# Converting the FFN weights inside tile 0 instead of ahead of it, and routing from the uncentred activations

## What is computed

```python
x = L0_attn_x
# block 1
h = ln(x);  spec = h @ W_to.T                     # 2*256 channels, real and imaginary
# per channel: state = state*decay + 0.1*u, rotated by a fixed angle, clipped to +-10
h = spectral_out @ W_from.T;  x2 = x + 0.1*h
h = gelu(ln(x2) @ W_ffn1.T + b1) @ W_ffn2.T + b2  # 4096 hidden
x = layernorm(x + (x2 + 0.1*h))
# block 2: mixture of experts, every expert computed densely, weighted by combine
logits = h @ router_weight.T                      # 8 columns
top_v, top_i = top_k(softmax(logits), 2);  top_v = top_v / top_v.sum()
gate, up = split(h @ gu.T);  out = silu(gate) * up @ dp.T
acc = acc + w[:, None] * out                      # over the 8 experts
x = layernorm(x + acc)
```

## Time and profile before

| | |
|---|---|
| runs shown | 5669.15 and 5701.72 us, median 5685.43 |
| profiled execution | 5680.6 us, span of its slowest core 5679.0 us |
| spans of the eight cores | 5626.9 to 5679.0 us |
| mean granted TensorE clock per core | 0.884 to 0.890 |
| TensorE, busy share of the span | 73% |
| VectorE, ScalarE, POOL | 35%, 18%, 8% |
| HBM | 641.87 MB read, 83.89 MB written |

### The profile page before, as it was taken

How to read it: one execution, slowest core, us unless ns; L and a number is a source line. 1 busy time by engine, 2 the same in 40 slices (tenths; PEclk the granted TensorE clock), 3 DMA queues, 4 the chain that set the end, 5 groups by cost and what they waited for, 6 DMA issues and landing times.

```text
span 5679.0 us, 55831 instructions; the slowest of 8 cores (5626.9 to 5679.0 us)
## 1 busy us (share of the span) xinstructions
PE 4162.6 (73%) x17824; PEld 1767.4 (31%) x17824; DVE 1979.9 (35%) x2879; ACT 1046.9 (18%) x1559; POOL 467.1 (8%) x391
## 2 busy tenths in 40 slices
PE   0028566665789768986789679987789578987797
PEld 0003222222334323332334233333334233433343
DVE  2032443222353324432353324431443325332333
ACT  0112311123111212112211212112201221122111
POOL 0000100000100002000100002000101001000210
PEclk9969788787899888997899789998899789988899
DMA  4722566662333242332333143332333233323242
GB/s 109 226 94 89 185 208 215 235 235 101 113 111 141 75 148 97 124 135 89 110 113 134 59 148 112 126 119 104 111 112 141 85 123 111 132 91 134 103 142 97
DMA packets 180314, 729.40 MB, mean 128 GB/s; under 512 B 28865, under 2 KB 28993, under 8 KB 112450
## 3 DMA queue, kind: packets, MB, share of 16 engines
...
HBM read 641.87 MB, written 83.89 MB: 128 GB/s over the span
## 4 chain that ended last, share of the span: by engine, by line
PE 63%; DVE 16%; DMA 6%; ACT 5%; SPq 5%; issue 3%; DVEq 1%; ACTq 1%; POOL 0%; POOLq 0%
PE PB L787 28%; PE PB L827 14%; PE PB L629 8%; PE PB L662 8%; SPq L257 4%; DMA RING<-guT 3%; ACT RING L286 2%; DVE ZS L442 2%; DVE PB L415 1%; DVE UPE L800 1%; PE PB L394 1%; PE PB L602 1%; DVE PRD L806 1%; DVEq L139 1%; DMA RING<-w1T 1%
## 5 line engine op out<-in xcount | busy, mean ns | idle before, releaser
L787 PE MATMUL PB<-BFIN,RING 128*128 128x512 bf16 x8192 | 1894.8, 394 | 173.3 <-ACT RING L286 113.4
L787 PEld LDWEIGHTS PB<-BFIN,RING 128*128 128x128 bf16 x8192 | 818.6, 101 | 1230.3 <-issue 372.8
L827 PE MATMUL PB<-PRD,RING 128*128 128x512 bf16 x4096 | 973.1, 400 | 226.9 <-DVE PRD L806 139.9
L629 PE MATMUL PB<-BFIN,RING 128*128 128x512 bf16 x2048 | 498.8, 404 | 388.2 <-DMA RING<-scr_w 223.8
L800 DVE TENSOR_TENSOR UPE<-PB,CBE 128x512 f32<-128x512 f32 x512 | 354.2, 692 | 1047.1 <-PE PB L787 969.4
L827 PEld LDWEIGHTS PB<-PRD,RING 128*128 128x128 bf16 x4096 | 412.7, 102 | 782.1 <-issue 360.6
L833 DVE TENSOR_TENSOR ACC<-PB,ACC 128x512 f32<-128x512 f32 x512 | 354.2, 692 | 693.3 <-PE PB L827 667.5
L806 POOL TENSOR_TENSOR PRD<-SG,UPE 128x512 bf16<-128x512 bf16 x256 | 297.1, 1160 | 2905.1 <-DVE UPE L800 2853.2
L794 ACT ACTIVATE SG<-PB 128x512 bf16<-128x512 f32 x512 | 303.6, 597 | 1034.9 <-PE PB L787 1027.5
L662 PE MATMUL PB<-G,RING 128*128 128x512 bf16 x2048 | 453.1, 379 | 0.0
L629 PEld LDWEIGHTS PB<-BFIN,RING 128*128 128x128 bf16 x2048 | 208.3, 102 | 677.2 <-issue 464.8
...
## 6 DMA issues: line engine op xcount, KB each, us to landing
...
RING<-scr_w SPq DMA_DIRECT2D x128, 1024.0 KB, 5.0
...
RING<-guT SPq DMA_DIRECT2D x256, 256.0 KB, 5.6
...
RING<-dpT SPq DMA_DIRECT2D x128, 256.0 KB, 5.4
...
```

Of the source, the lines that this page charges most:

```text
L629: mmm = opi("tensor", "T", lambda E, k=k, fc4=fc4, b=b, slot=slot: E.matmul(PB[b][:], slot[:, k * 512 + fc4 * 128: k * 512 + (fc4 + 1) * 1 ...
L787: mmm = opi("tensor", "T", lambda E, k=k, fc4=fc4, b=b, slot=slot, BFIN=BFIN: E.matmul(PB[b][:], slot[:, k * 512 + fc4 * 128: k * 512 + (f ...
L827: mmm = opi("tensor", "T", lambda E, k=k, oc4=oc4, b=b, slot=slot: E.matmul(PB[b][:], slot[:, k * 512 + oc4 * 128: k * 512 + (oc4 + 1) * 1 ...
```

## The change

Four things are changed.

1. `prewarm` is removed. The slabs of w1 and w2 are no longer converted ahead of tile 0; `emit_slab_load` finds no key for them in tile 0 and converts them there, inside FFN1 and FFN2, as it does for the expert slabs. The chain of tile 0 follows the router load directly.
2. In the twopass LN the squares go to the other activation buffer (`SQB`), and ScalarE no longer waits for the sum matmuls before it squares.
3. The router's matmuls take the uncentred bf16 cast in place of the normalized one. `RT` gets a ninth column of ones per chunk, which gives the token's sum; 32 matmuls of one column on the squares give the sum of squares. From these, eight small VectorE instructions and one small ScalarE square root make mean and reciprocal deviation per token and correct the logits by the column sums of the router weights (`SRB`, computed once at start-up with eight small matmuls). The ScalarE copy of the logits is gone. The POOL cast of the router weights becomes eight.
4. Pass 1 (the normalization into `BFIN`) is emitted behind the router's gating and not ahead of it. The first eight expert matmuls wait for it chunk by chunk.

At the end SyncE waits for all the DMA semaphores and not only for that of the output.

```diff
@@ -86,7 +87,7 @@
         CBE = sb("CBE", [128, T])
         WTO = sb("WTO", [128, KC * 512], BF16)
         WFR = sb("WFR", [128, 4 * 1024], BF16)
-        RT = sb("RT", [128, KC * NE], BF16)
+        RT = sb("RT", [128, KC * 9], BF16)
         RING = sb("RING", [128, 4 * 4096], BF16)
         ONESB = sb("ONESB", [128, 128], BF16)
         ONER = sb("ONER", [1, T], BF16)
@@ -99,6 +100,7 @@
         LDV = sb("LDV", [128, 2]); FRV = sb("FRV", [128, 2])
         DEC = sb("DEC", [128, 2]); PI2 = sb("PI2", [128, 1])
         LGS = sb("LGS", [128, 32])
+        SRB = sb("SRB", [128, 8])
         CMB = sb("CMB", [128, 32])
         CTE = sb("CTE", [8, T], BF16)
         MX4 = ZS[:, 0:32]; WW4A = ZS[:, 32:36]; WW4B = ZS[:, 36:40]
@@ -150,6 +152,9 @@
 
         def xc(buf, k, width=T):
             return buf[:, k * width:(k + 1) * width]
+
+        bank_free = [None] * 8
+        bank_ready = [None] * 8
 
         NRS = 4
         ring_free = [None] * NRS
@@ -326,8 +331,18 @@
         for kk in range(KC):
             ms_rt_rd = slot_dma(jr, lambda E, d=slot_r.bitcast(F32)[:, kk * 8:(kk + 1) * 8], s=rtR[kk]: E.dma_start(out=d, in_=s))
         w("gpsimd", ms_rt_rd)
-        ms_rt = opi("gpsimd", "G", lambda E, s=slot_r.bitcast(F32)[:, 0:64]: E.tensor_copy(out=RT[:], in_=s))
+        ms_rt = None
+        for kk in range(KC):
+            ms_rt = opi("gpsimd", "G", lambda E, kk=kk, s=slot_r.bitcast(F32)[:, kk * 8:(kk + 1) * 8]: E.tensor_copy(out=RT[:, kk * 9:kk * 9 + 8], in_=s))
         ring_set_free(jr, ms_rt)
+        ms_rto = opi("vector", "V", lambda E: E.memset(RT[:].rearrange("p (k e) -> p k e", k=KC)[:, :, 8], 1.0))
+        w("tensor", [ms_rt, ms_b2c, ms_rto])
+        ms_srb_mm = None
+        for kk in range(KC):
+            ms_srb_mm = opi("tensor", "T", lambda E, kk=kk: E.matmul(PB[6][:, 0:8], ONESB[:], RT[:, kk * 9:kk * 9 + 8], start=(kk == 0), stop=(kk == KC - 1)))
+        w("scalar", ms_srb_mm)
+        ms_srb = opi("scalar", "S", lambda E: E.activation(out=SRB[:], in_=PB[6][:, 0:8], func=AF.Copy))
+        bank_free[6] = ms_srb
 
         scr_ready = {}
 
@@ -354,8 +369,6 @@
 
 
 
-        bank_free = [None] * 8
-        bank_ready = [None] * 8
 
         def emit_slab_load(dram_ap, key):
             if key not in scr_ready:
@@ -383,6 +396,10 @@
             cast_ms = [None] * KC
             sq_ms = [None] * KC
             mmS_ms = [None] * KC
+            SQB = BFINS[1 - bfin_p] if twopass else BFIN
+            sq_p = (1 - bfin_p) if twopass else bfin_p
+            if twopass:
+                w("scalar", bfin_user[sq_p])
             for k in range(KC):
                 if per_chunk:
                     w("scalar", src_ready[k])
@@ -393,16 +410,19 @@
             for k in range(KC):
                 mmS_ms[k] = opi("tensor", "T", lambda E, k=k: E.matmul(PB[0][:], ONESB[:], xc(BFIN, k), start=(k == 0), stop=(k == KC - 1)))
             for k in range(KC):
-                w("scalar", mmS_ms[k])
-                sq_ms[k] = opi("scalar", "S", lambda E, k=k: E.activation(out=xc(BFIN, k), in_=src(k), func=AF.Square))
+                if not twopass:
+                    w("scalar", mmS_ms[k])
+                sq_ms[k] = opi("scalar", "S", lambda E, k=k: E.activation(out=xc(SQB, k), in_=src(k), func=AF.Square))
             w("tensor", bank_free[1])
             mmQ_last = None
             for k in range(KC):
                 w("tensor", sq_ms[k])
-                mmQ_last = opi("tensor", "T", lambda E, k=k: E.matmul(PB[1][:], ONESB[:], xc(BFIN, k), start=(k == 0), stop=(k == KC - 1)))
+                mmQ_last = opi("tensor", "T", lambda E, k=k: E.matmul(PB[1][:], ONESB[:], xc(SQB, k), start=(k == 0), stop=(k == KC - 1)))
             bank_ready[0] = mmS_ms[KC - 1]
             bank_ready[1] = mmQ_last
-            bfin_user[bfin_p] = mmQ_last
+            bfin_user[sq_p] = mmQ_last
+            if twopass:
+                bfin_user[bfin_p] = None
             w("vector", bank_ready[0])
             opi("vector", "V", lambda E: E.tensor_scalar(out=MEANT[:], in0=PB[0][:], scalar1=float(1.0 / D), scalar2=None, op0=OP.mult))
             opi("vector", "V", lambda E: E.tensor_tensor(out=ZS[:, 0:T], in0=MEANT[:], in1=MEANT[:], op=OP.mult))
@@ -417,12 +437,16 @@
             f_ms = [None] * KC
             if twopass:
                 w("vector", st.get("p2_done"))
-                opi("vector", "V", lambda E: E.tensor_copy(out=RSTD[:], in_=PB[1][:]))
-                for k in range(KC):
-                    opi("vector", "V", lambda E, k=k: E.tensor_tensor(out=ZS[:, 0:T], in0=src(k), in1=MEANT[:], op=OP.subtract))
-                    bf_ms[k] = opi("vector", "V", lambda E, k=k: E.tensor_tensor(out=xc(BFIN, k), in0=ZS[:, 0:T], in1=PB[1][:], op=OP.mult))
-                bank_free[0] = bf_ms[KC - 1]
-                bank_free[1] = bf_ms[KC - 1]
+                ms_rstd = opi("vector", "V", lambda E: E.tensor_copy(out=RSTD[:], in_=PB[1][:]))
+                st["p1_stats"] = ms_rstd
+
+                def pass1():
+                    for k in range(KC):
+                        opi("vector", "V", lambda E, k=k: E.tensor_tensor(out=ZS[:, 0:T], in0=src(k), in1=MEANT[:], op=OP.subtract))
+                        bf_ms[k] = opi("vector", "V", lambda E, k=k: E.tensor_tensor(out=xc(BFIN, k), in0=ZS[:, 0:T], in1=PB[1][:], op=OP.mult))
+                    bank_free[0] = bf_ms[KC - 1]
+                    bank_free[1] = bf_ms[KC - 1]
+                st["p1_pass1"] = pass1
 
                 def p2_step(k):
                     def go():
@@ -436,7 +460,8 @@
                             st["p2_done"] = f_ms[k]
                     return go
                 st["p1_pass2_steps"] = [p2_step(k) for k in range(KC)]
-                return bf_ms[KC - 1], None, sq_ms[KC - 1], bf_ms, f_ms
+                st["p1_sq"] = sq_ms
+                return cast_ms, None, sq_ms[KC - 1], bf_ms, f_ms
             w("vector", extra_vwait)
             for k in range(KC):
                 opi("vector", "V", lambda E, k=k: E.tensor_tensor(out=ZS[:, 0:T], in0=src(k), in1=MEANT[:], op=OP.subtract))
@@ -680,19 +705,6 @@
         prev_out_so = [None]
         pending_p2 = [None]
 
-        def prewarm(key):
-            if key in scr_ready:
-                return
-            srcs, dram = _scr_srcs(key)
-            _, mw, jo, _ = prepass_unit(srcs, dst_dram=dram)
-            scr_ready[key] = mw
-            ring_set_free(jo, mw)
-
-        for _fr in range(8):
-            prewarm(("w1", _fr))
-        for _sl in range(8):
-            prewarm(("w2", _sl))
-
         for s in make_chain(0):
             s()
 
@@ -711,18 +723,44 @@
             BFIN = BFINS[i % 2]
             w("tensor", bank_free[6])
             if i == 0:
-                w("tensor", ms_rt)
+                w("tensor", [ms_rt, ms_srb, ms_rto])
             lg_last = None
             for tg in range(4):
                 for k in range(KC):
                     if tg == 0:
-                        w("tensor", p1_bf[k])
+                        w("tensor", ms_p1bf[k])
                     lg_last = opi("tensor", "T", lambda E, tg=tg, k=k, BFIN=BFIN: E.matmul(
-                        PB[6][:, tg * 8:(tg + 1) * 8], xc(BFIN, k)[:, tg * 128:(tg + 1) * 128], RT[:, k * 8:(k + 1) * 8],
+                        PB[6][:, tg * 9:(tg + 1) * 9], xc(BFIN, k)[:, tg * 128:(tg + 1) * 128], RT[:, k * 9:(k + 1) * 9],
                         start=(k == 0), stop=(k == KC - 1)))
-            w("scalar", lg_last)
-            ms_lgs = opi("scalar", "S", lambda E: E.activation(out=LGS[:], in_=PB[6][:, 0:32], func=AF.Copy))
-            w("vector", ms_lgs)
+            SQB2 = BFINS[(i + 1) % 2]
+            for tg in range(4):
+                for k in range(KC):
+                    if tg == 0:
+                        w("tensor", st["p1_sq"][k])
+                    lg_last = opi("tensor", "T", lambda E, tg=tg, k=k, SQB2=SQB2: E.matmul(
+                        PB[6][:, 36 + tg:37 + tg], xc(SQB2, k)[:, tg * 128:(tg + 1) * 128],
+                        RT[:, 8:9],
+                        start=(k == 0), stop=(k == KC - 1)))
+            P63 = PB[6][:, 0:36].rearrange("p (g c) -> p g c", g=4)
+            w("vector", lg_last)
+            opi("vector", "V", lambda E: E.tensor_scalar(out=CBE[:, 0:4], in0=P63[:, :, 8], scalar1=float(1.0 / D), scalar2=None, op0=OP.mult))
+            opi("vector", "V", lambda E: E.tensor_tensor(out=CBE[:, 8:12], in0=CBE[:, 0:4], in1=CBE[:, 0:4], op=OP.mult))
+            opi("vector", "V", lambda E: E.scalar_tensor_tensor(out=CBE[:, 4:8], in0=PB[6][:, 36:40], scalar=float(1.0 / D), in1=CBE[:, 8:12], op0=OP.mult, op1=OP.subtract))
+            ms_veps2 = opi("vector", "V", lambda E: E.tensor_scalar(out=CBE[:, 4:8], in0=CBE[:, 4:8], scalar1=float(EPS), scalar2=None, op0=OP.add))
+            w("scalar", ms_veps2)
+            ms_sq2 = opi("scalar", "S", lambda E: E.activation(out=CBE[:, 4:8], in_=CBE[:, 4:8], func=AF.Sqrt))
+            w("vector", ms_sq2)
```

(20 more changed lines are left out.)

1 line of the change is left out of this document (added).

## The result

| | before | after |
|---|---|---|
| all executions of the first timing, median | 5772.54 us (10) | 5807.76 us (11) |
| lowest and highest of them | 5666.68, 6220.44 | 5537.76, 6089.67 |
| ratio of the undisturbed executions (one of 5616 us among them), first timing | | 0.9784 [0.9706, 0.9862] |
| the same, second timing (after_again) | | 0.9739 [0.9700, 0.9778] |
| profiled execution | 5680.61 us | 5539.51 us |

There the change saves 2.2% and 2.6% in the two timings; the first interval reaches from 1.4 to 2.9% and alone would not show that it is over 2%, the second, 2.2 to 3.0%, does. The profiled execution is 141 us shorter.

A forecast was written before the change was run, and what follows sets the result against it. TensorE computes 73% of the span, so its idle time matters: the conversion standing alone and each tile's LN and router stretch. 111 + 28 = 139 us off the profiled 5680.6 gives 5542, range 5510 to 5588.

The forecast's parts named there:

- How the numbers follow: Closing step on the whole time: predicted 5542 us, range 5510 to 5588, with 0.3% spread between executions.
- rival 3: FFNs of tiles 1 to 7: dense stretches fall to clock 0.81, 27 us more each, time 5730; chance 0.03.
- Part A: Start and tile 0: dropping the conversion ahead hides tile 0's FFN under its own conversion, gain 111 us.
- The reasoning on the cover: Tile 0's FFN: the wait for DMA covers TensorE's work; a slab's compute beyond its interval would lengthen the stretch.
- intervals reach 16 us: Tile 0's FFN: store intervals this long, against about 14 us expected, would show the forecast wrong.
- Part B: LN and router stretch of all eight tiles: the new order gains 3.5 us per tile, 28 us in all.
- eight small ops and the Sqrt: Router statistics on DVE's path: 2.4 us for the small ops and 0.4 for the Sqrt, 2.8 added.
- dense experts sooner: Tile 1 after the router: dense expert matmuls begin at 1512.7, 2.0 us sooner than before.
- clock after the dense start: Start of the experts: clock at 0.50 in either kernel, so that cost moves but stays.
- Rival 1: Tile 0's FFN: TensorE at 1.2 GHz takes 13.5 us a slab and sets the rhythm; time 5575; chance 0.13.
- Rival 2: Router stretch: late small matmuls and dear small ops eat the gain, Part B 0, time 5569; chance 0.12.
- Rival 4: Tile 0's conversion: quicker rhythm of 12.9 us a slab, or gain above the middle; time 5523; chance 0.12.

The follow-up runs named there:

- after_again: The changed kernel itself, unaltered, timed once more beside the kernel before on one chip; 5530, 5506 and 5511 us beside 5658, ratio 0.9739.
- a_only: The kernel before with the standing-alone conversion of w1 and w2 removed, nothing else; 5539 and 5523 us beside 5659, ratio 0.9777.
- sums_late: The changed kernel with the column sums of the router weights emitted behind chain 0 instead of ahead of it; ratio 0.9715 to the kernel before.
- b_only: The changed kernel with the conversion of w1 and w2 put back ahead of tile 0; 5617, 5633, 5626 and 5662 us, ratio 0.9959.
- pass1_first: The changed kernel with pass 1 emitted ahead of the gating again, raw router kept; 5564, 5556 and 5541 us, ratio 0.9817.
- after_b: The changed kernel itself, timed again on another occasion; 5520 and 5513 us beside 5666 for the kernel before.
- ffn1_more_mm: The changed kernel with 124 more full-size matmuls in FFN1 of tile 0; FFN ends at 443 to 458 us on six cores, 476 and 481 on two.
- store_later: The changed kernel with each converted slab's store issued behind the next slab's first read, in tile 0; 5459, 5467 and 5460 us, ratio 0.9644.

## Why the prediction was right and wrong

**The recorded time lies outside the range.** The step that failed is "How the numbers follow". Its range 5510 to 5588 was added up from costs alone, and what one execution differs from the next was put at 0.3%, from the two runs shown and the profile. The measured median of all executions is 5808 us, and that of the kernel before 5773, because long executions stand in the middle of both: 7 of the 12 of the changed kernel were long, 5 of the 10 of the kernel before. In the later timings 23 of 42 of the kernel before were, and 35 of 71 of the others, so nothing shows that the change has a part in it. A trace shows what such an execution is. The profiled one of after_again took 5820 us, and there core 2 runs the FFN of tile 2 at granted 1.00 and that of tile 6 at 0.81 (columns as above):

```profile
1945.00:1995.00 50.00, 49.74 (x223) 21.61 (x227) 5.98 (x9) 2.53 (x4) 0.00 (x0) 1.00 0.25 87
4540.00:4590.00 50.00, 49.65 (x185) 19.89 (x188) 5.53 (x8) 2.53 (x4) 0.00 (x0) 0.81 0.23 84
```

That is the loss of rival 3, in some executions of either kernel and not brought by the change; why an execution has it is open. In the others the forecast 5542 stands beside 5540, 5535, 5540 and 5538 us, and beside 5616 where one die had 0.865.

**Part A, 111 us forecast.** In the profiled core 112.3 (566.05 to 453.8), by the medians of eight cores 111 (554 to 443). Term by term: chain 0's first cast 98 forecast, 97.25 found; first store 233.3 and 234.3; interval 14.14 and 13.9; last slab 9.5 and 9.8; end 455.0 and 453.8. The reasoning on the cover holds, with less room over TensorE than I had said. The sign "intervals reach 16 us" came for the first three of w1 (17.5, 16.4 and 16.1 us in the profiled core), but the conversion that stood alone had 17.1 at its start too, so a cold TensorE is not their cause. What the sum does not tell is what a_only and sums_late showed: 15 to 17 us of what moving the conversion gives are lost. I had written that chain 0 "can start once the router column sums are copied by ACT" and put its start at 98; I compared that with the old start behind the conversion and never with the start that it could have. The term was sized right and its cause, a new wait in ACT's list, was not called a cost.

**Part B, 28 us forecast.** In the profiled pair the way from the FFN's end of tile 0 to the last matmul is 5086.2 before (566.0 to 5652.2) and 5056.6 after (453.8 to 5510.4): 29.6 us. a_only and b_only, which differ in nothing else there, give 4.8 us a tile instead of 3.5. That the pair's 29.6 lies so close to the forecast is in part luck: core 3 spent 136 us at granted 0.81 after and 76 before, in tiles 1 to 7, and in a_only and b_only none. The terms of tile 1:

| term | forecast | measured |
|---|---|---|
| start of the squares | 0.6 | 0.7 |
| 64 router matmuls | hidden, 2.1 us or more | hidden, 2.9 us |
| eight small ops and the Sqrt | 2.8 | 2.6 |
| dense experts sooner | 2.0 | 2.4 |
| matmuls done ahead | 7, 1.5 us | 7, 1.5 us |
| clock after the dense start | same | 0.3 to 0.5 us less |

The last term was wrong in kind. I had said that the 1.2 GHz stretch at the experts' start "moves but stays". In the ten us after the dense start the time at granted 0.50 is 4.0 to 6.0 us in the seven tiles of the kernel before (median 5.2), and 3.3 to 5.7 in the changed kernel (median 4.1), both in core 3; over all cores the medians are 4.9 and 4.2. Windows of two us in tile 1, columns as above, of the changed kernel and then of the kernel before:

```profile
1399.80:1401.80 2.00, 2.00 (x6) 0.73 (x5) 0.00 (x0) 0.53 (x1) 0.64 (x1) 0.50 0.00 0
1401.80:1403.80 2.00, 2.00 (x10) 0.87 (x9) 0.00 (x0) 0.71 (x2) 0.00 (x0) 0.99 0.03 8
```

```profile
1518.70:1520.70 2.00, 2.00 (x7) 0.65 (x5) 0.00 (x0) 1.54 (x2) 0.00 (x0) 0.51 0.00 0
1520.70:1522.70 2.00, 2.00 (x11) 0.94 (x10) 0.00 (x0) 0.60 (x1) 0.00 (x0) 1.00 0.00 0
```

2.4 GHz is there 4 us after 1397.78 in the one and 6 us after 1514.68 in the other. The seven paced matmuls ahead are not needed for it: pass1_first has none, TensorE stands idle for 26.7 us before its gating's transposes, and there the median over all cores is 3.5 us. What sets this time is open.

**The rivals.** Rival 1 (cold slabs) came about in single slabs (core 4 of after_b) and not on the whole; ffn1_more_mm brought it on. Rival 2 (router work eats its gain) would have been true without the new place of pass 1. Rival 3 (dense stretches lose clock) did not come with the change: in both profiled executions the last 80 us of every FFN of tiles 1 to 7 run at granted 1.00 on all eight cores, that of tile 1 in this row:

```profile
1288.00:1303.00 15.00, 15.00 (x71) 6.83 (x70) 0.00 (x0) 5.64 (x10) 0.00 (x0) 1.00 0.39 144
```

By the Trainium skill's rule (TensorE: Matmul & The Clock Gate, the note on the peak-current limiter) this dense stretch on all cores would run at 13/16. It does not, here or in the kernel before. In the profiled execution of after_again the level of the rule is there, 0.81, on cores 2 and 3 in the FFNs of tiles 5 to 7 and on cores 0 and 1 in those of tiles 1 and 2, while the other tiles from 1 on do the same work at 1.00. The level agrees and the condition does not, so the measurement decides. Rival 4 (a quicker rhythm) did not come by itself; store_later had to make it.
